# Causal masks of an attention stage moved from PE's products to VectorE's maxima and GpSimd's selections

## The reference

```python
scores = jnp.einsum('bhqd,bhkd->bhqk', q, k)
causal = jnp.tril(jnp.ones((S, S), dtype=bool))
scores = jnp.where(causal, scores, -jnp.inf)
probs = jax.nn.softmax(scores, axis=-1)
attn = jnp.einsum('bhqk,bhkd->bhqd', probs, v)
```

## Time and profile before

| | |
|---|---|
| median of 3 runs (lowest, highest) | 768.18 us (766.91, 771.41) |
| the profiled execution's own time | 766.19 us |
| its span in the profile | 764.4 us |
| busy: PE, PEld | 601.8 us (79%), 399.8 us (52%) |
| busy: VectorE, ScalarE, GpSimd | 479.9 us (63%), 276.2 us (36%), 263.1 us (34%) |
| attention, first scores to last products | about 375 to 604 us |
| expert blocks | about 611 to 750 us |

### The profile page before, as it was taken

How to read it: one execution, slowest core, us unless ns; L and a number is a source line. 1 busy time by engine, 2 the same in 40 slices (tenths; PEclk the granted TensorE clock), 3 DMA queues, 4 the chain that set the end, 5 groups by cost and what they waited for, 6 DMA issues and landing times.

```text
span 764.4 us, 10605 instructions
## 1 busy us (share of the span) xinstructions
PE 601.8 (79%) x3606; PEld 399.8 (52%) x3606; DVE 479.9 (63%) x1060; ACT 276.2 (36%) x535; POOL 263.1 (34%) x242
## 2 busy tenths in 40 slices
PE   3933667877676869999459998888878799999991
PEld 2721335655552758888225555455445456666660
DVE  6869997969768765695497777877774211221223
ACT  1376433223110212345207664554435432222220
POOL 3157467745265743447572001001016011111111
PEclk9975669989867999999659999999999999999996
DMA  6101200000011200168995663260003892000005
GB/s 186 53 27 55 79 2 0 1 1 0 0 39 42 74 10 1 55 122 161 193 266 78 85 85 50 37 84 2 3 15 115 332 421 87 21 21 28 22 21 178
DMA packets 43619, 58.35 MB, mean 76 GB/s; under 512 B 7184, under 2 KB 37072, under 8 KB 42544
## 3 DMA queue, kind: packets, MB, share of 16 engines
q1 hardware_dynamic: 41696, 52.55, 28.9%
q0 software_dynamic: 1872, 5.13, 1.9%
HBM read 41.97 MB, written 15.51 MB: 75 GB/s over the span
## 4 chain that ended last, share of the span: by engine, by line
PE 38%; DVE 10%; DMA 3%; issue 2%; ACT 2%; POOL 1%; SPq 0%; POOLq 0%; DVEq 0%; ACTq 0%
PE bank L745 19%; DVE small L1679 4%; PE bank L992 4%; PE bank L969 4%; PE bank L942 4%; PE bank L739 4%; DMA pieces<-P 2%; PE bank L944 1%; PE bank L971 1%; POOL P L2094 1%; DVE mtok L1690 1%; PE bank L1009 1%; DMA yt<-results 1%; ACT PTa L1265 1%; DVE XA L1708 0%
## 5 line engine op out<-in xcount | busy, mean ns | idle before, releaser
L1679 DVE TENSOR_REDUCE small<-bank 128x1 f32<-128x256 f32 (+3 forms) x256 | 107.3, 482 | 9.1 <-PE bank L944 8.1
L745 PE MATMUL bank<-wall,xt 128*128 x184 | 82.8, 593 | 0.0
L1999 POOL TENSOR_TENSOR al<-hm,ah 128x512 fp32r<-128x512 f32 (+1 forms) x28 | 40.9, 1462 | 91.4 <-ACT ah L1228 91.4
L942 PE MATMUL bank<-Ks,Qs 96*128 96x256 bf16 (+3 forms) x256 | 67.2, 330 | 5.3 <-DVE small L1679 3.7
L1938 DVE TENSOR_TENSOR bhm<-bsg,bank 128x512 f32<-128x512 f32 x23 | 15.8, 687 | 83.9 <-PE bank L745 83.9
L969 PE MATMUL bank<-Qs,Ks 99*128 99x512 bf16 (+3 forms) x256 | 58.8, 306 | 5.0 <-issue 4.6
L944 PE MATMUL bank<-maskb,identb 128*128 128x128 bf16 x256 | 55.6, 236 | 0.0
L1550 DVE TENSOR_TENSOR_SCAN S<-AT,U 128x512 f32<-128x512 f32 x32 | 49.7, 1554 | 8.2 <-POOL QS L2017 7.9
L1265 ACT ACTIVATE PTa<-bank 128x512 f32<-128x512 f32 (+1 forms) x96 | 43.6, 528 | 29.5 <-PE bank L971 29.2
L1265 ACT ACTIVATE PTb<-bank 128x512 f32<-128x512 f32 (+1 forms) x96 | 43.7, 529 | 28.9 <-PE bank L971 28.5
L745 PEld LDWEIGHTS bank<-wall,xt 128*128 128x128 f32 x184 | 33.2, 190 | 33.0 <-issue 33.0
(11 more groups left out here) (344 smaller groups left out, 1513.6 us busy)
## 6 DMA issues: line engine op xcount, KB each, us to landing
wall<-e_pack SPq DMA_DIRECT2D x8, 1536.0 KB, 15.2
pieces<-P SPq DMA_DIRECT2D x12, 512.0 KB, 9.9
Qs<-pieces SPq DMA_DIRECT2D x48, 128.0 KB, 5.4
Ks<-pieces SPq DMA_DIRECT2D x48, 128.0 KB, 6.0
stg<-w_pack SPq DMA_DIRECT2D x18, 256.0 KB, 2.7
wf<-t_pack SPq DMA_DIRECT2D x12, 256.0 KB, 2.6
sorted_rows<-blank SPq DMA_DIRECT2D x1, 2944.0 KB, 13.9
yt<-results SPq DMA_DIRECT2D x8, 256.0 KB, 4.7
```

The lines of the kernel that those rows point to most:

```text
L745: last = nc.tensor.matmul(outap, a, b_, start=start and i == 0, stop=stop and i == n - 1, **kw)
L942: nc.tensor.matmul(banks[b][:, o:o + w], Q[0:96, h, i * P:(i + 1) * P], K[0:96, h, 0:w], start=True, stop=False)
L1679: last = nc.vector.tensor_reduce(mxv[:, i, h:h + 1], banks[b][:, o:o + w], AX.X, ALU.max, negate=True)
L1999: nc.gpsimd.tensor_tensor(al[0:M, s % 3, :], hm[0:M, s % 3, :], ah[0:M, s % 3, :].bitcast(F32), ALU.subtract).then_inc(*alr.tick(s))
```

## The change

Neither pass has mask products any more. `maxima` uses VectorE's `tensor_tensor_reduce`: it adds a mask of up to 512 columns (zeros, and the triangle in the last 128) to the tile, writes the sum back to the same PSUM tile and gives the maximum, no longer negated; `max_parts` negates instead. The mask lies where the q and k bias was, and VectorE builds it behind the projections (item `("mask",)`). The transposed scores stay unmasked; behind the exponentials of a head GpSimd sets what lies above the diagonal to zero, by two `affine_select` (three blocks, and the fourth that lies elsewhere in the tile), and `attend` waits for these (`cut`) and not for the exponentials. The rows of ones come from a 3 x 512 memset by two DMAs that SP issues, the first ahead of the first pieces, the second ahead of the loads of the output weights. The bf16 mask is gone.

```diff
         ORDER += [("mask",), ("xb", 1), ("w", "wo1"), ("w", "wr"), ("w", "wo0")]      # was: ("xb", 1), ("ones", 1), ..., ("ones", 2)
...
+            def ones_rows(slot):
+                sp.dma_start(stacks[slot][1][96:99, :, :], L1["ones_row"][0:3, :].unsqueeze(1).broadcast_to([3, H, CH]))\
+                    .then_inc(s_ones[slot], 16)
+            sp.wait_ge(*ones_set.upto("row"))
+            ones_rows(0)
             write_pieces(0)
...
             sp.wait_ge(*mm.upto(("v", N_TILES // 2 - 1)))
+            ones_rows(1)
             for j in range(LAST_JOB["qkv0"] + 1, len(JOBS)):
...
-                        nc.tensor.matmul(banks[b][:, o:o + w], Q[0:96, h, i * P:(i + 1) * P], K[0:96, h, 0:w],
-                                         start=True, stop=False)
-                        last = nc.tensor.matmul(banks[b][:, o + w - P:o + w], identb[:], maskb[:], start=False, stop=True)
+                        last = nc.tensor.matmul(banks[b][:, o:o + w], Q[0:96, h, i * P:(i + 1) * P], K[0:96, h, 0:w],
+                                                start=True, stop=True)
...
-                    pe.wait_ge(*ones_set.upto(n % 2))
+                    pe.wait_ge(s_ones[n % 2], 16)
...
-                        nc.tensor.matmul(banks[b][:, o:o + w], K[0:99, h, j * P:(j + 1) * P], Q[0:99, h, j * P:CH],
-                                         start=True, stop=False)
-                        last = nc.tensor.matmul(banks[b][:, o:o + P], maskb[:], identb[:], start=False, stop=True)
+                        last = nc.tensor.matmul(banks[b][:, o:o + w], K[0:99, h, j * P:(j + 1) * P], Q[0:99, h, j * P:CH],
+                                                start=True, stop=True)
...
-                    for i_ in range(3):
-                        pe.wait_ge(*ex.upto((4 * q + 3, i_)))
+                    for i_ in range(2):
+                        pe.wait_ge(*cut.upto((4 * q + 3, i_)))
...
-                        last = nc.vector.tensor_reduce(mxv[:, i, h:h + 1], banks[b][:, o:o + w], AX.X, ALU.max, negate=True)
+                        s_ = banks[b][:, o:o + w]
+                        last = nc.vector.tensor_tensor_reduce(s_, s_, wide_mask[:, CH - w:CH], 1.0, LOWEST, ALU.add, ALU.max,
+                                                              mxv[:, i, h:h + 1])
...
-                link(nc.vector.tensor_copy(tv(0), mq))
-                link(nc.vector.tensor_tensor(r, mq, tv(0), ALU.subtract))
+                link(nc.vector.tensor_scalar(tv(0), mq, -1.0, None, ALU.mult))
+                link(nc.vector.scalar_tensor_tensor(r, mq, -1.0, tv(0), ALU.mult, ALU.subtract))
...
+                elif op == "mask":
+                    tell(nc.vector.memset(wide_mask[:, 0:CH - P], 0.0))
+                    link(nc.vector.tensor_copy(wide_mask[:, CH - P:CH], maskf[:]))
...
+                        nc.gpsimd.memset(L1["ones_row"][0:3, :], 1.0).then_inc(*ones_set.tick("row"))
...
-                        nc.gpsimd.memset(stacks[slot][1][96:99, :, :], 1.0).then_inc(*ones_set.tick(slot))
...
+                elif op == "st":
+                    g = it[1]
+                    pt = L1["PTa" if g // 4 % 2 == 0 else "PTb"][:, g % 4, :]
+                    pool.wait_ge(*ex.upto((g, 2)))
+                    v = pt.rearrange("p (b n) -> p b n", n=2 * P)[:, 0:5:2, 0:P]
+                    nc.gpsimd.affine_select(v, v, [[0, 3], [1, P]], ALU.is_ge, 0.0, base=0, channel_multiplier=-1)\
+                        .then_inc(*cut.tick((g, 0)))
+                    v = pt[:, PT_AT[3]:PT_AT[3] + P]
+                    nc.gpsimd.affine_select(v, v, [[1, P]], ALU.is_ge, 0.0, base=0, channel_multiplier=-1)\
+                        .then_inc(*cut.tick((g, 1)))
```

More of the change, by code:

```diff
@@ L50 @@
 NEG = -1.0e30
+LOWEST = -3.0e38
 PIECE_Q = (0, 0, 1, 1, 0, 2)
@@ L142, in build @@
         identb = sb("identb", [P], BF16)
-        maskb = sb("maskb", [P], BF16)
         vec = sb("vec", [16], F32)
@@ L222, in build @@
         pta, o = plan([("PTa", [4, 1280], F32)], mlp_at)
-        l1d, _ = plan([("spare", [BLOCKS, 2], F32), ("ranks", [6, NE], F32), ("by_rank", [NE, NE], F32), ("load_i", [NE], I32),
-                       ("places", [2, BLOCKS], F32), ("place_i", [BLOCKS], I32)], o)
+        l1d, o = plan([("spare", [BLOCKS, 2], F32), ("ranks", [6, NE], F32), ("by_rank", [NE, NE], F32), ("load_i", [NE], I32),
+                       ("places", [2, BLOCKS], F32), ("place_i", [BLOCKS], I32), ("ones_row", [CH], BF16)], o)
+        assert o <= mlp_at + 22528
         moe, _ = plan([("wall", [NE * EW], F32)], region + 4608)
@@ L281, in build @@
         s_stack = [[sem(f"stack{i}_half{j}_loaded") for j in range(2)] for i in range(2)]
+        s_ones = [sem("ones_rows0_placed"), sem("ones_rows1_placed")]
         s_out = sem("output_written")
@@ L333, in build @@
         ex = tally("probabilities")
+        cut = tally("probabilities_cut")
         pv = tally("attention_sums")
@@ L498, in build @@
             ORDER += beside.get(u, [])
-        ORDER += [("xb", 1), ("ones", 1), ("w", "wo1"), ("w", "wr"), ("w", "wo0"), ("ones", 2)]
+        ORDER += [("mask",), ("xb", 1), ("w", "wo1"), ("w", "wr"), ("w", "wo0")]
         ST_LAG = 8
@@ L558, in build @@
         ORDER += [("sum", h) for h in range(NT // 2)]
+        wide_mask = bias[:, D:D + CH]
         def spare(c, i):
@@ L588, in rows_part @@
             return [i < e for _b, e in XG_PARTS].index(True)
+        PT_AT = [0, 512, 1024, 896]
         block = ctx.enter_context(nc.Block())
@@ L968, in scores_t @@
                         w = (4 - j) * P
-                        nc.tensor.matmul(banks[b][:, o:o + w], K[0:99, h, j * P:(j + 1) * P], Q[0:99, h, j * P:CH],
-                                         start=True, stop=False)
-                        last = nc.tensor.matmul(banks[b][:, o:o + P], maskb[:], identb[:], start=False, stop=True)
+                        last = nc.tensor.matmul(banks[b][:, o:o + w], K[0:99, h, j * P:(j + 1) * P], Q[0:99, h, j * P:CH],
+                                                start=True, stop=True)
                         o += w
                     last.then_inc(*mm.tick(("st", g, i_)))
-            PT_AT = [0, 512, 1024, 896]
             def attend(q, j):
@@ L1812, in _ @@
                     nc.vector.tensor_copy(identb[:], ident[:]).then_inc(*setup.tick("identb"))
-                    nc.vector.tensor_copy(maskb[:], maskf[:]).then_inc(*setup.tick("maskb"))
                     nc.vector.tensor_copy(flat(L0["sel"]), flat(L0["wf"])[:, 0:8 * P]).then_inc(*setup.tick("sel"))
@@ L2080, in _ @@
                             .then_inc(*blank_set.tick("tokens"))
[L2081 to L2086, removed]
-                        nc.gpsimd.memset(stacks[slot][1][96:99, :, :], 1.0).then_inc(*ones_set.tick(slot))
-                        pool.wait_ge(*ones_set.upto(slot))
                 elif op == "qk" and tile(it[1])[0] == 0:
```

## The result

The changed kernel takes 779.1 us (median of four runs, 776.7 to 781.2) where the kernel before takes 767.8 beside it: ratio 1.0134, 95% interval 1.0108 to 1.0159. The forecast was 776.8 us within 759 to 790. The profiled execution took 779.04 us, its span 777.3 us: 12.9 us more than the span before. The profiled execution was forecast at 774.8 us.

A forecast was written before the change was run, and what follows sets the result against it. PE bounds attention, VectorE already setting part of the pace. -0.4 (start) - 1 + 0 - 1 (heads) + 1 (ports) + 10 (end) = +8.6: 766.19 becomes 774.8, median 776.8 us, range 759 to 790.

The forecast's parts named there:

- The queue on GpSimd: End of attention: scattering DMAs and late heads' cuts wait behind one another on GpSimd; together +10 us at the end.
- the two cold stretches of PE: End of attention: PE's work runs slower after each of two idle waits; estimated +1.4 us for both.
- One sign: End of attention: PE idle 4 to 6 us ahead of L954 and again ahead of quad 14's products.
- The new maxima: VectorE's masked maxima: each costs 0.07 us more than a reduction, 0.28 us a head; bounds 0 and 0.17 us.
- The sum for a plain quad: Plain stretch of attention: VectorE's 9.3 us plus 0.7 us of waiting make 10.0 us a quad, no gain.
- the one without any extra: Plain quad if a maximum costs what a reduction costs: 9.2 us; that rival gave 766 us, chance 0.2.
- Products gone, 461 to 570 us: Heads among output projections and router: 7.4 us of masks come off, dearer maxima take most back; gain 1 us.
- First heads and plain quads: Heads 0 to 7 (401 to 421 us) gain 1 us; 3.5 plain quads gain 0.
- Cuts: GpSimd's two cuts a head: 0.51 and 0.30 us, hidden except after the last head, +0.9 us.
- Meetings on the shared port: Small VectorE operations, four a quad, meet GpSimd's cuts on the shared port pair; +1 us over all quads.
- Rows of ones: Start: both memsets and a 4.4 us VectorE stall go, but SP's loads had hidden it; gain 0.4 us.
- The sum: Whole kernel: +8.6 us, profiled execution from 766.19 to 774.8 us, median 776.8 us.

The follow-up runs named there:

- e4: Changed kernel with the scores' masks made by products and the maxima by plain reductions, cuts everywhere; 777.69 us, ratio 1.0114.
- e11: e4 with the transposed masks of heads 52 to 63 made by products, cuts only for heads 0 to 51; 766.57 us, ratio 0.9978.
- e5: Changed kernel with plain reductions over unmasked scores for the maxima, cuts kept; 775.4 us, ratio 1.0106.
- e7: Changed kernel with plain reductions over unmasked scores and the transposed masks of heads 52 to 63 by products; 764.0 us, ratio 0.9942.
- e2: Changed kernel with the transposed masks of heads 52 to 63 made by products again, no cuts there; median 775.5 us, ratio 1.0082.
- e6: Changed kernel with both masks by products and plain reductions again; ones by DMA and an unused wide mask stay; 769.72 us, ratio 1.0019.
- e8: Changed kernel with both masks made by products as before, the new maxima kept on top, no cuts; 774.75 us, ratio 1.0079.
- e9: The kernel of e2 executed once more, unchanged, for another trace; 768.86 us, a single execution.
- e1: Changed kernel with GpSimd's order alone changed, scattering DMAs (puts) moved ahead of cuts; 779.27 us, ratio 1.0147.
- e3: Changed kernel with all transposed masks made by products and no cuts, new maxima kept; 775.16 us, ratio 1.0084.
- e10: The kernel of e3 executed once more, unchanged, for another trace; 775.89 us, a single execution.
- e12: e7 with the rows of ones written by GpSimd's two memsets again instead of two DMAs; 764.67 us, ratio 0.995.

## Why the prediction was right, and where it was not

**The queue on GpSimd** was the main term, and it held step by step. Counted from the slots: put 0 starts after 6.9 us (forecast 6.9) and ends after 17.0 (17.0); VectorE's copy of the shares comes after 18.6 (19.0); put 1 ends after 29.7 (30.2); quad 14's products come after 32.9 (33.8), the last quad's after 42.0 (41.0, and 42.4 with the two cold stretches of PE). +9.7 us against +10. The runs confirm it by taking it away: e4 to e11 is 11.1 us, e5 to e7 11.4, each in the median and as much behind the slots (11.1 and 11.0). Only between the changed kernel and e2 the median gives 3.6, though both traces of that kernel show the 9 to 10 us. One sign did not come as forecast: PE was to be idle 4 to 6 us twice and was idle 2.61 us ahead of L967 and 2.71 ahead of quad 14's products. In front of the first of these its own work was slower, at a granted clock of 0.55 from 571 to 586 us (0.93 in the same place before), and filled part of the wait.

**The new maxima** were forecast at 0.07 us extra and cost 0.05 (distance of starts) or 0.04 (pace of e5): the record of 0.14 us overlaps the next instruction. In the range from 0 to 0.17 the nearest row was half as much again too high. The Trainium skill (VectorE: DVE Perf Modes, Two Vector instructions with no wait between them) has two instructions for such a maximum; the trace agrees, with two records each. The sum for a plain quad, 10.0 us, came out 9.65, and the one without any extra, 9.2, came out 9.0. The mechanism, VectorE in the place of PE as the bound, is borne out by the paces: taking the scores' products out is worth 0.3 us a quad (e11 to e7, same cheap maxima), while making the maxima dear costs 0.65 (e5 to after).

**Products gone, 461 to 570 us:** here a step failed. It read: 7.4 us of masks come off, 3.6 and 3 us of VectorE come on, gain 1. Up to the slots, +3.7 us were measured. The runs price the terms apart. VectorE's was too large: 3.7 (e6 to e8) in place of 6.6. The masks' was far too large: taking both kinds away brings, with the new maxima, from e8's 120.0 to 117.3, 119.7, 120.0 and 120.5 (e9, e1, after, e2), 0.6 us in the mean; with plain ones, from e6's 116.3 to 113.7 and twice 115.8, 0.5 to 2.6. These are sizes from single traces, and two executions of one kernel differ by 2.5 us (e3, e10) and 3.2 us (e2, e9) in this stage; the median of many executions bears out the first (5.0 us from e6 to e8, all stages), and the second, for e2 has 464 products fewer than e8, the same maxima and no queue, and takes 775.5 us against 774.8. A share of the chain was taken for a gain. The time that PE no longer spends on masks it spends waiting for VectorE, and part of it at the lower clock: busy time times clock in that window is 92.8 x 0.98 = 91 us before and 85.2 x 0.89 = 76 us after, so that by this estimate 15 us of full-speed work went and only 7.5 us of busy time with it. PE's timeline of the changed kernel shows where it falls:

```profile
478.25 0.39 PE L967 MATMUL bank<-identb,mtok 128*12 128x128 bf16 x4 [1.23 <-DVE mtok L1705]
...
479.54 1.25 PE L956 MATMUL bank<-Ks,Qs 96*128 96x128 bf16 x3 [0.37 <-DVE small L1690]
480.73 1.91 PE L1002 MATMUL bank<-PTa,Va 128*17 128x512 f32 x8
482.57 1.25 PE L982 MATMUL bank<-Qs,Ks 99*128 99x512 bf16 x4
```

From 461 to 480 us PE was busy 13.35 of 19 us (15.92 before); behind that the granted clock of the next 20 us is 0.78, with part of them at 1.2 GHz: the eight products take 1.91 us where the kernel before, without such a fall, took 1.05:

```profile
481.60 1.05 PE L992 MATMUL bank<-PTa,Va 128*17 128x512 f32 x8
```

The forecast had this loss at the end of attention only. What makes the clock fall is not shown: PE was busy 16.03 us from 461 to 480 in e10, more than in the kernel before, and its clock behind that was 0.74. Nor is the low clock needed for the 120.0 us, as e8 shows.

**First heads and plain quads** were forecast at -1 and 0, and -1.2 us came together, by luck: from the first transposed scores to the quad at 422 us it is 0.2 us less (20.3 against 20.5), and the other 1.0 comes from three plain quads. **Cuts** take 0.524 and 0.295 us, forecast 0.51 and 0.30, and are hidden elsewhere. **Meetings on the shared port**: from 421 to 570 us the four small operations of a quad take 0.20, 0.18, 0.20 and 0.20 us, where each takes 0.17 when nothing is beside it; over eleven quads 1.1 us longer in these instructions, forecast 1; what of it reached the time is not shown.

**Rows of ones:** a gain of 0.4 us was forecast; the start came 0.6 us later instead, and e6 (0.9 us slower than before, 0 to 3 by the interval) and e12 against e7 (0.7 slower with the memsets) point opposite ways, neither clear of nothing. That most of the stall was hidden is shown by e12: some 10 us of it were put back, and the 0.7 us do not stand out of the spread of the two kernels. The Trainium skill (SBUF — State Buffer, Who interferes with whom) keeps the lock to instructions on that port pair, and e12's rows agree: the 13 reductions out of PSUM, about half of them beside the first memset, take 0.42 us each as elsewhere, and the 16-column operation behind them waits for the memset's end.

**The sum.** The median was forecast 2.3 us too low, the profiled execution 4.2 (774.8 against 779.04). The difference is luck: the forecast carried over the 2.0 us by which the profiled execution before lay under its median, and that of the changed kernel does not lie under its own. The 12.9 us against 8.6 are 1.0 at the start and 3.7 from 452 us to the slots, where the heads' gain and the ports were to cancel.

**What stays open.** e2 and e3 spread over 10 us between executions, the kernels with plain maxima over 6 to 8, the kernel before over 8 (765.0 to 773.0) in the many executions taken beside these runs. The longer executions of e3 have the low mean clocks (0.893 to 0.895 at 767.8 and 768.8 us, 0.878 to 0.885 at 777 us and above), but e8 takes 774.8 us at a good clock. No trace was taken of an execution of e2 above 772 us, so where its other 6 us go is not shown. Nor is it known why the first transposed scores move between 401.3 and 405.7 us from one trace to another, for of the kernel before there is one trace only.

## What to carry to other kernels

Work that is moved to an idle engine joins that engine's queue: look up what stands ahead of it there at the one moment when the others wait, and keep the old form for those few steps (e11, the change's cuts everywhere but in the last three quads, turned 777.7 us into 766.6). A line's share of the chain is what it could give if nothing else were next; where the second engine is level, price the engine that stays, since 0.04 to 0.05 us on each of 256 VectorE instructions cost 5.0 us (e6 to e8), nearly what taking 464 of PE's 512 mask products away brought (5.7, e6 to e7). If a maximum serves only to keep exponentials in range, it need not be masked at all, provided that no masked score can exceed its row's own by so much that the row's exponentials vanish; e7 uses that and is the fastest kernel here (764.0 us), and where it can't be granted, e11 is still 0.2% faster than before.

## What was not expected of the hardware

- Reading the accumulator of a VectorE instruction with two outputs has a record of 0.139 us, yet a maximum with it costs only 0.04 to 0.05 us more than a reduction.
- With PE's products gone the granted clock from 461 to 570 us falls from 0.98 to 0.89, and a stretch of 20 us full of work runs at 0.78 (17.4 us busy). With 0.74 in the same place e10 is 2.5 us later at the slots than e3 with 0.91.
- A 16-column operation on VectorE waited 6.82 us for a memset of 6.92 us on GpSimd (e12), nearly its whole length; the first heads came 1.6 us later than in e7, and the median is 0.7 us longer.
